# Order of the score sums, bias adds, probability sums and last exponential in a fused two-layer kernel on Trainium2

## The reference

```
xn = layernorm(x);  x = x + attn0(xn) + ffn0(xn)
xn = layernorm(x);  x = x + attn1(xn) + ffn1(xn)
```

## Time and profile before

| | |
|---|---|
| median of 3 runs | 355.44 us (355.14 to 356.28) |
| profiled execution | 355.92 us, span 354.1 us |
| PE, busy | 304.5 us (86%) |
| PEld | 252.0 us (71%) |
| DVE | 311.0 us (88%) |
| ACT | 178.9 us (51%) |
| POOL | 250.2 us (71%) |
| mean granted clock of TensorE | 0.979 |

### The profile page before, as it was taken

How to read it: one execution, slowest core, us unless ns; L and a number is a source line. 1 busy time by engine, 2 the same in 40 slices (tenths; PEclk the granted TensorE clock), 3 DMA queues, 4 the chain that set the end, 5 groups by cost and what they waited for, 6 DMA issues and landing times.

```text
span 354.1 us, 5666 instructions
## 1 busy us (share of the span) xinstructions
PE 304.5 (86%) x1771; PEld 252.0 (71%) x1771; DVE 311.0 (88%) x826; ACT 178.9 (51%) x499; POOL 250.2 (71%) x162
## 2 busy tenths in 40 slices
PE   0568877899898987589999999899998999989995
PEld 0246555777686776477877887698987888878785
DVE  4995899979879677976999999899998999989795
ACT  3345766778786767677242531613516235162520
POOL 4184667826557361117999899989999899988671
PEclk9996999999999999879999999999999999999999
DMA  5590000000000000004853332423424334253102
GB/s 142 161 302 9 2 0 1 2 1 1 3 0 3 0 0 3 0 4 122 182 128 93 102 105 90 118 61 91 149 82 111 120 94 115 59 148 114 38 2 59
DMA packets 21321, 24.91 MB, mean 70 GB/s; under 512 B 2420, under 2 KB 12060, under 8 KB 21292
## 3 DMA queue, kind: packets, MB, share of 16 engines
q1 hardware_dynamic: 20248, 24.09, 24.7%
q10 hardware_dynamic: 820, 0.39, 0.4%
q0 software_dynamic: 224, 0.08, 0.1%
HBM read 22.19 MB, written 2.36 MB: 69 GB/s over the span
## 4 chain that ended last, share of the span: by engine, by line
DVE 37%; PE 34%; POOL 12%; issue 10%; ACT 6%; DMA 1%; DVEq 0%; POOLq 0%; ACTq 0%
PE Q L944 16%; PE VN L944 8%; PE T L944 7%; POOL prod_qk L874 6%; POOL prod_pv L884 4%; DVE hid L1632 4%; DVE rope_b L1368 3%; DVE rope_a L1366 3%; DVE att L1591 2%; PE T L940 2%; DVE sgc L1619 2%; DVE scr L1577 2%; DVE bst L1209 2%; DVE attn L1398 2%; DVE xT_lo L1419 1%
## 5 line engine op out<-in xcount | busy, mean ns | idle before, releaser
L874 POOL TENSOR_TENSOR prod_qk<-qkv 128x1024 f32<-128x1024 f32 x32 | 76.6, 2412 | 2.9 <-DVE above L1461 2.1
L884 POOL TENSOR_TENSOR prod_pv<-prob,qkv 128x1024 f32<-128x1024 f32 x32 | 69.0, 2195 | 7.4 <-DVE att L1591 5.1
L773 ACT ACTIVATE Q<-Q 128x512 f32<-128x512 f32 x48 | 27.5, 581 | 56.5 <-PE Q L944 56.3
L1632 DVE TENSOR_TENSOR hid<-T,sgc 128x512 f32<-128x512 f32 x64 | 43.4, 679 | 0.1
L944 PE MATMUL Q<-bias,ones 128*128 128x400 f32 (+1 forms) x64 | 30.3, 474 | 15.2 <-ACT v_ext L663 7.1
L1577 DVE TENSOR_REDUCE scr<-prod_qk 128x128 f32<-128x1024 f32 x32 | 38.8, 1211 | 5.0 <-POOL prod_qk L874 5.0
L944 PEld LDWEIGHTS Q<-w,hid 128*128 128x128 f32 x288 | 37.5, 191 | 3.4 <-DVE hid L1632 0.6
L944 PEld LDWEIGHTS VN<-w,hid 128*128 128x128 f32 x288 | 37.6, 191 | 3.1
L944 PE MATMUL Q<-w,hid 128*128 128x128 f32 x288 | 38.0, 275 | 0.4 <-DVE hid L1632 0.4
L944 PE MATMUL T<-xT_hi,w_hi 128*128 128x512 f32 x72 | 31.2, 434 | 8.2 <-DVE hid L1632 7.9
L1591 DVE TENSOR_REDUCE att<-prod_pv 128x128 f32<-128x1024 f32 x32 | 38.2, 1195 | 0.0
(11 more groups left out here) (186 smaller groups left out, 801.1 us busy)
## 6 DMA issues: line engine op xcount, KB each, us to landing
cw<-comb_table SPq DMA_DIRECT2D x62, 256.0 KB, 4.6
out_x<-fin SPq DMA_DIRECT2D x7, 256.0 KB, 4.5
x<-in_x SPq DMA_DIRECT2D x2, 256.0 KB, 3.1
wraw<-in_w1T SPq DMA_DIRECT2D x1, 512.0 KB, 4.2
w3raw<-in_w3T SPq DMA_DIRECT2D x1, 512.0 KB, 4.9
w<-in_w2T SPq DMA_DIRECT2D x1, 512.0 KB, 5.9
cw<-comb_table SPq DMA_DIRECT2D x4, 128.0 KB, 3.1
rope_s<-in_c_sin ACTq DMA_DIRECT2D x1, 256.0 KB, 5.1
```

The costliest lines, as they stand in the source:

```text
L773: act.activation(gated[:, :], gate_bank(n, s)[:, :], ACT.Silu).then_inc(sg_ready, 1)
L874: pool.tensor_tensor(prod_qk[:, t % 2], bc(qkv2[:, TH * half + t, j, 0:D], 1, NB), qkv2[:, :, j, D:2 * D], ALU.mult).then_inc(qk_prod, 1)
L884: pool.tensor_tensor(prod_pv[:, t % 2].rearrange("p (h e) b -> p b h e", e=HD), bc(prob[:, t].rearrange("p h b -> p b h"), 3, HD), qkv2[:, ...
L1632: V.tensor_tensor(hid[:, s % 3, :], UB[k][:, :], src, ALU.mult)\
```

## The change

- Score sums: a unit that begins less than nine slices after the one before (`short`: units 3, 5 and 7) has its four score sums at p = -7, -6, -1, 0. Before, units 3 and 5 had them at -8, -7, -2, -1 like the others; unit 7 is as before. In each case that is the first two and the last two slices between two bases, moved back by one slice for units 3 and 5; the fourth sum then stands in the slice of the maximum, ahead of it.
- Sum of probabilities: at p = 3, ahead of the first value sum, for all units (before at p = 5, for the last at 2). Reciprocal: at p = 4, behind the second value sum (before at p = 6 ahead of the fourth, for the last at 3).
- Bias: a call adds the bias to the four batches and the position tile of one unit (before: to all four tiles of one batch). Calls 0 and 1 stand before unit 0 as before; calls 2 to 5 stand in units 3 to 6 between the next unit's first product and less_max (before: calls 2 to 7 in units 0 to 5, same place); call 6 ahead of the last unit's normalise and call 7 behind it. `residual` of unit n waits for n + 1 calls (before 4 or 8).
- The last unit's exponential: at p = 2 like the others (before p = 1), so in slice 66 instead of 65.

```diff
                 for u, p in units(k):
-                    if p == (1 if u == END else 2):
+                    if p == 2:
                         exp_done(u)
...
-            def biased(c):
-                if c == 0:
+            def biased(n):
+                j, half = place(n)
+                b = slice(TH * half, TH * half + TH)
+                if n == 0:
                     pool.wait_ge(ld_w2, 64)
-                pool.wait_ge(xn2_ready, 2 * c + 2)
-                pool.tensor_tensor(x[:, c], x[:, c], bc(bout2[:, :], 1, NJ), ALU.add).then_inc(x_biased, 1)
+                    pool.wait_ge(xn2_ready, 2 * TH)
+                if n == TH:
+                    pool.wait_ge(xn2_ready, 2 * NB)
+                pool.tensor_tensor(x[:, b, j, :], x[:, b, j, :], bc(bout2[:, :], 1, TH), ALU.add)\
+                    .then_inc(x_biased, 1)
...
                 next_qk(0)
-                if n + 2 < NB:
-                    biased(n + 2)
+                if 3 <= n < END:
+                    biased(n - 1)
                 less_max(n)
                 next_qk(1)
                 products_pv(n, n % NJ)
                 next_qk(2)
                 next_qk(3)
+                if n == END:
+                    biased(END - 1)
                 normalise(n)
+                if n == END:
+                    biased(END)
...
-                dve.wait_ge(x_biased, TH * half + TH)
+                dve.wait_ge(x_biased, n + 1)
...
-                first = (-4, -3, -2, -1) if u == 0 else (-7, -6, -1, 0) if u == END else (-8, -7, -2, -1)
+                short = u > 0 and BASE[u] - BASE[u - 1] < NS
+                first = (-4, -3, -2, -1) if u == 0 else (-7, -6, -1, 0) if short else (-8, -7, -2, -1)
...
-                if p == (2 if u == END else 5):
+                if p == 3:
                     sum_of_p(u)
-                if p == (3 if u == END else 6):
-                    over_sum(u)
                 if 3 <= p < 3 + TH:
                     values(u, p - 3)
+                if p == 4:
+                    over_sum(u)
```

## The result

The changed kernel takes 356.41 us (median of 17 runs), the kernel before 355.20 (17 runs): ratio 1.0039, 95% interval 1.0024 to 1.0054. The forecast was 0.8 later, measured are 1.2 by the medians and 1.4 (0.9 to 1.9) by the ratio. The profiled execution took 355.93, its span 354.1, as much as before by chance: the part up to the `hid` of slice 5 was 1.2 us shorter (175.5 for 176.7). That part varies by as much between profiles whatever the edit: 175.3 to 176.9 in the four with the old bias adds, 175.4 to 177.5 in the ten with the new.

| from ...

What follows compares the result with a forecast made beforehand. Three nearly full engines in the second layer, so waits between them count. A loss of 2.5 at the end less 1.7 gained upstream is 0.8 later: 356.2 us on the median of 355.44, range 354.2 to 357.4 (8 in 10).

Steps and rivals of the forecast that it cites:

- Direction and its cause: Slice 66 on ScalarE: the last Exp lands behind unit 6's attention copy, Silu 67 comes late; 2.5 us lost, 0.8 in total.
- the forecast's 8.6: VectorE's work from the weighting of slice 67 to the last value sum, sum of probabilities included: 8.6 us.
- Upstream gain: Up to the last maximum: gains 1.16, 1.1 and 0.67, losses 0.2, 0.5, 0.4 and 0.1; 1.7 us gained.
- the four stalls: VectorE's waits before second score sums in slices 33, 42, 50 and 58: 0.8, 0.2, 1.15 and 1.4 us.
- its step on the score sums: Units 3 and 5, sums a slice later: stalls of slices 24 and 41 shrink, gains 1.16 and 1.1, loss 0.2 us.
- Bias: GpSimd's bias adds by unit: those dropped from units 0 to 2 gain 0; unit 6's add costs 0.1 us.
- Silu of slice 34: VectorE's wait for this Silu goes because earlier `hid` bring copy and Silu some 1.1 us sooner: gain 0.67.
- Behind the last value sum nothing changes: End of the kernel: normalise, transposes, copy, product, last add and store take as long as before: 0.
- 1: Rival: the last exponential is not held by the copy, gain of 1.2 instead of the loss, 352.5 us; chance 0.10.
- 2: Rival: GpSimd is in time for less_max in units 3 to 6, those stalls go, 354.3 us; chance 0.13.
- 3: Rival: TensorE does not follow VectorE, gains of slices 24 and 34 are gone, 357.4 us; chance 0.13.
- Its signs: Expected profile marks in stalls and ScalarE's order; forecast falls if slice 64's `hid` ends at 332.5 or 329.5, not some 330.9.

Runs made afterwards that it cites:

- e1: The changed kernel with the last unit's exponential put back in slice 65: 354.01 us, ratio 0.9959 to the kernel before.
- e3: The kernel before with only the last unit's exponential moved from slice 65 to 66: 357.47 us, ratio 1.0051.
- e8: The e7 kernel with unit 6's attention copy a slice later (slice 67, behind Silu 67): 350.33 us, ratio 0.9860 to the kernel before.
- e5: The kernel before with only the score sums of units 3 and 5 a slice later: 353.55 us, ratio 0.9942.
- e12: The kernel before with only the bias adds changed (by unit, in units 3 to 6 and the last): 354.96 us, ratio 0.9997.
- e7: The changed kernel with the bias adds of units 3 and 5 moved, so calls 2 to 5 stand in units 1, 2, 4, 6: 354.29 us, ratio 0.9974.
- e6: The kernel before with only the sums of probabilities at p = 3 and reciprocals at p = 4: 355.95 us, ratio 1.0016.
- e9: The changed kernel unaltered, run again beside one with extra TensorE products on the same chip: 356.13 us, ratio 1.0034 to the kernel before.
- e2: The changed kernel with the last exponential still in slice 66 but issued ahead of unit 6's copy: 353.95 us, ratio 0.9962 to the kernel before.

## Why the prediction was right, and where it was not

- *Direction and its cause: right, and shown.* Exp behind the copy, as read from the order of the loop, costs 2.49 where 2.5 was forecast, and the weighting of slice 67 starts 6.85 behind the end of slice 64's `hid`, as summed. e1 takes the loss away, e3 brings 1.9 of it with the moved exponential alone (the rest is the sum of probabilities, which the forecast's 8.6 holds too), e8 removes the copy from between.
- *Upstream gain: right in sum (1.90 for 1.7), in part by luck.* With the overlap of 0.08 the four stalls are 0.86, 0.24, 1.24 and 1.37 for 0.8, 0.2, 1.15 and 1.4. That they cost 0.16 more than forecast is made up by the wait for Silu 51 (0.2), which stands in no term. For slice 33 the prediction named the wait that the changed kernel shows, that of the third value product (0.63 at 230.01). But its step on the score sums missed a second hold: unit 3's third score sum, moved a slice back, keeps GpSimd's buffer. In e5 that alone makes the same stall, so leaving the sums of probabilities where they were would not have saved the 0.5. Score sums alone gain 2.4, the earlier sums of probabilities take back 0.5 of it (0.86 where they stand alone).
- *Bias: right* (e12: nothing). That the add costs time where GpSimd is late is confirmed by e7.
- *Silu of slice 34: right.* Counted from the `hid` of slice 5 it starts at 71.7 in the changed kernel and in e5, at 73.9 before: 2.3 sooner, while the `hid` of slice 31, behind unit 3's maximum, is 1.1 sooner. In e6 the wait is gone too, but by another way: the Silu is no sooner (74.0), and VectorE comes 0.6 later through the stall of slice 33.
- *"Behind the last value sum nothing changes": wrong* by 0.60 in the profiled execution, where TensorE at the lower clock is late for the transposes. In e9 nothing changes there, and the three stretches come to 0.65, a little under the forecast 0.8. That its median, like that of the first 17 runs, still lies higher fits executions that lose the clock; how many do is open.
- *Rivals.* 1 did not happen in the change, and its price belongs to e8's order, not to Exp merely put ahead (e2). 2 needed the adds moved (e7). 3 did not happen: TensorE followed.
- *Its signs.* All held but one as it was worded: the `hid` of slice 64 ends at 329.49 (328.81 and 0.68), near the 329.5 at which the forecast was to fall. That is 3.1 sooner, but 1.2 of it lie ahead of slice 5; counted from there it is the 1.90.

## What to carry to other kernels

Before an instruction is moved into another step of an in-order queue, list what else that step holds for the same engine: here a copy whose wait reached through TensorE to VectorE cost more than the wait that the move removed. An instruction that needs no table can still keep a table load waiting, since the load stands right ahead of its user. Where three engines are nearly full, filler work such as a bias add belongs where its engine is shown to wait, and two of its adds in the wrong place cost 1.8 us.

## What was not expected of the hardware

The granted clock of TensorE fell to 0.57 for four microseconds in one profiled execution of the changed kernel after idle stretches of 0.70 and 1.36 us, and stayed at 1.00 after the same two stretches in two others (e7, e9). At the lower clock eight products of 128 columns took 1.86 instead of 1.05 us.
